# Cross attention scores on one Trainium2 core: full-height products against pairs of half-height products

## What is computed

```
q = xn2 @ Wq_c + bq_c                 # per sequence 16 heads x 1024 x 32
k = ctx @ Wk_c + bk_c                 # per sequence 16 heads x   64 x 32
v = ctx @ Wv_c + bv_c
scores = (q @ k.T) / DH ** -0.5       # 16 heads x 1024 x 64
attn = softmax(scores, axis=-1)
x = x + (attn @ v) @ W2 + b2
```

## Time and profile before

| | us |
|---|---|
| median of 3 runs (lowest, highest) | 2375.3 (2372.14, 2384.62) |
| the profiled execution: its time | 2376.49 |
| the profiled execution: its span | 2374.7 |
| TensorE (matmuls) busy | 2223.8 (94%) |
| weight loads busy, beside the matmuls | 1606.6 (68%) |
| VectorE, ScalarE, GpSimd busy | 1414.0, 867.5, 934.5 |
| mean granted TensorE clock, share of full speed | 0.971 |

### The profile page before, as it was taken

How to read it: one execution, slowest core, us unless ns; L and a number is a source line. 1 busy time by engine, 2 the same in 40 slices (tenths; PEclk the granted TensorE clock), 3 DMA queues, 4 the chain that set the end, 5 groups by cost and what they waited for, 6 DMA issues and landing times.

```text
span 2374.7 us, 31670 instructions
## 1 busy us (share of the span) xinstructions
PE 2223.8 (94%) x11334; PEld 1606.6 (68%) x11334; DVE 1414.0 (60%) x3348; ACT 867.5 (37%) x1598; POOL 934.5 (39%) x943
## 2 busy tenths in 40 slices
PE   6999999999999999878999998999999999999996
PEld 4665565556555655436777776788887887788784
DVE  4377757775777566745666667553446545554636
ACT  3145645554556455443333434221112121121213
POOL 1057666666677667773433333110112202021212
PEclk9999999989999999799999999999999999999998
DMA  7265544544455346321121112321111111211011
GB/s 231 29 90 85 104 66 78 92 91 66 77 96 97 66 78 96 104 72 49 68 80 54 58 54 76 116 85 54 36 67 58 67 62 54 94 54 67 32 36 49
DMA packets 106321, 177.31 MB, mean 75 GB/s; under 512 B 18334, under 2 KB 23454, under 8 KB 106160
## 3 DMA queue, kind: packets, MB, share of 16 engines
q1 hardware_dynamic: 106164, 175.29, 31.0%
HBM read 83.67 MB, written 40.13 MB: 52 GB/s over the span
## 4 chain that ended last, share of the span: by engine, by line
PE 75%; DVE 9%; issue 6%; ACT 4%; POOL 3%; DMA 2%; SPq 0%; POOLq 0%; ACTq 0%; DVEq 0%
PE psum L55 18%; PE psum L56 17%; PE psum L57 17%; PE psum L793 5%; PE psum L743 5%; PE psum L781 4%; PE psum L701 1%; PE psum L802 1%; DVE psum L995 1%; POOL es L658 1%; PE psum L754 1%; ACT sx L1342 1%; DMA ks<-stage 1%; PE psum L1296 1%; PE psum L720 1%
## 5 line engine op out<-in xcount | busy, mean ns | idle before, releaser
L658 POOL TENSOR_TENSOR es<-es,er 128x512 f32<-128x512 f32 (+3 forms) x640 | 589.6, 958 | 346.4 <-PE psum L793 305.8
L891 ACT ACTIVATE er<-psum 128x512 f32<-128x512 f32 (+3 forms) x640 | 279.8, 470 | 327.7 <-DVE psum L1006 191.4
L995 DVE CUSTOM_DVE_ANT_0 psum<-psum,mask_ts 128x384 f32<-128x384 f32 (+3 forms) x512 | 248.7, 502 | 231.3 <-PE psum L743 230.1
L743 PE MATMUL psum<-ks,qs 96*128 96x512 f32 (+3 forms) x768 | 270.8, 378 | 22.4 <-DMA ks<-stage 11.0
L781 PE MATMUL psum<-qs,ks 100*128 100x512 f32 (+3 forms) x768 | 261.9, 375 | 18.3 <-DVE mx L999 9.9
L1846 ACT ACTIVATE fy<-psum,cols 128x512 f32<-128x512 f32 x128 | 88.2, 689 | 453.2 <-PE psum L57 452.6
L743 PEld LDWEIGHTS psum<-ks,qs 96*128 96x128 f32 x768 | 145.6, 197 | 123.4 <-issue 48.8
L999 DVE TENSOR_REDUCE mx<-psum 128x1 f32<-128x512 f32 x256 | 175.4, 685 | 68.2 <-PE psum L743 67.6
L781 PEld LDWEIGHTS psum<-qs,ks 100*128 100x128 f32 x768 | 145.7, 196 | 92.5 <-DVE mx L999 24.2
L55 PE MATMUL psum<-fh,hh 128*128 128x512 f32 x512 | 201.1, 393 | 7.1 <-DVE hl L1947 7.1
L55 PE MATMUL psum<-fah,fh 128*128 128x512 f32 x512 | 203.4, 397 | 0.0
(11 more groups left out here) (257 smaller groups left out, 4507.4 us busy)
## 6 DMA issues: line engine op xcount, KB each, us to landing
qs<-stage SPq DMA_DIRECT2D x96, 256.0 KB, 5.6
ks<-stage SPq DMA_DIRECT2D x96, 256.0 KB, 6.7
rs<-rs_d SPq DMA_DIRECT2D x32, 256.0 KB
sa_d<-rs SPq DMA_DIRECT2D x32, 256.0 KB, 2.1
sx<-sa_d SPq DMA_DIRECT2D x8, 1024.0 KB, 5.6
xt<-in_x SPq DMA_DIRECT2D x32, 256.0 KB, 5.9
x_d<-xt SPq DMA_DIRECT2D x32, 256.0 KB, 2.0
fw<-in_Wf SPq DMA_DIRECT2D x16, 512.0 KB, 5.3
```

The lines of the kernel that those rows point to most:

```text
L658: e.tensor_tensor(es, es, er, ALU.add).then_inc(s_add.sem, 1)
L743: t = e.matmul(bank1(*s)[:, v * wd:v * wd + wd], Q.qs[par][0:96, i, 128 * ti:128 * ti + 128], Q.ks[par][0:96, i, c0:c0 + wd], start=True, ...
L891: e.activation(dst, bank1("sc", g, c2, j, i)[:, off:512], ACT.Exp, scale=SCALE).then_inc(s_freeS.sem, 1)
L995: t = e.tensor_tensor_reduce(out=ps, in0=ps, in1=mask_ts[:, 512 - wd:512], scale=1.0, scalar=-3e38, op0=ALU.add, op1=ALU.max, accum_out=mx ...
```

## The change

Each score product over 128 partitions and 256 columns becomes two over 64 partitions and 128 columns each. Half `a` (partitions 64a to 64a+63) holds heads 2a and 2a+1 of the group, its block diagonal is 128 columns wide, and its scores go to bank 3 + a, at columns 128m. The two halves are issued in turn. `kbh` and `kbl` are half as wide, and a gap of 4096 floats per partition keeps all later buffers where they were. Since the banks now hold the heads in another order, `place(h)` gives the place of head h, and the transposes of `2tu` read `pp` from there. All waits, increments and planned times stay as they were.

```diff
-            R.kbh = sb(ctx, "kbh", [128, NB, 4, 256], F32R)
-            R.kbl = sb(ctx, "kbl", [128, NB, 4, 256], F32R)
+            R.kbh = sb(ctx, "kbh", [128, NB, 4, 128], F32R)
+            R.kbl = sb(ctx, "kbl", [128, NB, 4, 128], F32R)
+            sb(ctx, "gap2", [128, 4096])
...
+        def place(h):
+
+            return 8 * (h // 2 % 2) + 2 * (h // 4) + h % 2
...
-                t = three(e, bank[3 + m // 2][:, 256 * (m % 2):256 * (m % 2) + 256], (R.qh[qp][:, m, r], R.ql[qp][:, m, r]),
-                          (R.kbh[:, b, m, :], R.kbl[:, b, m, :]), True, True)
+                for z, (lhs, rhs) in enumerate(((R.qh, R.kbh), (R.qh, R.kbl), (R.ql, R.kbh))):
+                    for a in range(2):
+                        pair = slice(64 * a, 64 * a + 64)
+                        t = e.matmul(bank[3 + a][:, 128 * m:128 * m + 128], lhs[qp][pair, m, r], rhs[pair, b, m, :], start=z == 0, stop=z == 2)
...
-                    h = 2 * (4 * hf + v)
+                    h = place(2 * (4 * hf + v))
...
-                    e.activation(R.kbh[r, :, m, 64 * i:64 * i + 64], bank[(1 + m) % 2][r, 0:256].rearrange("p (b s) -> p b s", s=S),
+                    e.activation(R.kbh[r, :, m, 64 * (i % 2):64 * (i % 2) + 64], bank[(1 + m) % 2][r, 0:256].rearrange("p (b s) -> p b s", s=S),
...
-                    dh, dl = (q[r, :, m, 64 * i:64 * i + 64] for q in (R.kbh, R.kbl))
+                    dh, dl = (q[r, :, m, 64 * (i % 2):64 * (i % 2) + 64] for q in (R.kbh, R.kbl))
```

## The result

The changed kernel takes 2384.75 us (median of 20 runs, 2372.03 to 2393.10), the kernel before 2378.64 us in as many runs beside it (2365.39 to 2384.62): ratio 1.0030, 95% interval 1.0019 to 1.0042. That is 7 us, between 4.5 and 10: slower by a hair, within what was called no change. The forecast was 2385 us and a loss of 9.5 us. That 2385 was met to 0.3 us is luck: the forecast started from 2375.3 us, and the kernel before took 3.3 us more beside the changed one, which made up for a loss some 3 us smaller than forecast. The loss is what the forecast is to be judged by.

What follows compares the result with a forecast made beforehand. The prediction took TensorE as the bound: 32 short runs +11.2 us, their pairs -1.9, runs of 12 +0.2, together +9.5 on the median of 2375.3, giving 2385 us; range 2370 to 2421.

Steps and rivals of the forecast that it cites:

- What is worked on: Score products between 1095 and 1510 us: 12 per tile at 0.120 us, 32 tiles, 46 us or 1.9% of the kernel.
- A pair in 0.11 us: Two half products with their loads take 0.11 us, 0.01 less than the full product; 192 pairs in short runs: -1.9 us.
- 0.35 us per run: Entering and leaving a run of half products costs 0.35 us; 32 short runs, not covered: +11.2 us.
- Runs of 12 covered by their stalls: In 16 tiles with one run of 12, leaving falls into TensorE's existing stall of some 0.47 us; taken: +0.2 us.
- The sum, +9.5 us: All terms together: 9.5 us added to the median of 2375.3 us, giving 2385 us.
- lower end: Forecast case's range, 2379 to 2390 us; its low side allows part to fall into TensorE's waits for GpSimd and ScalarE.
- a microsecond added to TensorE is a microsecond of the kernel: TensorE, busy 94% of the span, is the bound; added time counts fully unless it falls where TensorE waits.
- Clearing and filling: Clearing `kbh` and `kbl` takes about 1.75 us each instead of 3.5; filling the diagonals is unchanged; both gain nothing.
- Loads queue: Rival: the two halves' loads use one path, a pair takes 0.22 us; total +44 us, 2420 us; chance 0.27.
- No change over: Rival: a split by partitions costs nothing to enter; -4 us, 2371 us; chance 0.12.
- free of the load: Rival: a pair takes only its columns' 0.06 us; -23 us, 2352 us, or 2363 with change overs; chance 0.04.
- Doesn't do what it says: Rival: halves run without any overlap, or the change over costs double, 0.7 us per run; +22 us, 2397 us; chance 0.10.

Runs made afterwards that it cites:

- the lower half twice: Changed kernel with the upper half's products replaced by the lower half's, made a second time into the upper half's bank: 2423.2 us, ratio 1.0201.
- one run per tile: Changed kernel with the four score steps of each tile planned next to one another, 32 runs of score products instead of 48: 2380.6 us, ratio 1.0013.
- high by high only: Two remainder products left out, 4 score products or pairs per tile instead of 12: kernel before 2365.0 us (0.9965), changed kernel 2374.0 us (0.9996).
- the half kernel: Changed kernel with each tile's score steps planned together, right before the value products: 2409.4 us (1.0139); kernel before on the same plan 2391.6 us (1.0069).

## Why the prediction was right

- **What is worked on.** "46 us is all that the change works on": held; outside the stretch nothing moved that doesn't move between profiles of one kernel or of kernels with full products too.
- **A pair in 0.11 us.** Held, by the timeline (0.11) and by the sum over runs. It was taken from column splits and applies to row splits. That it rests on the loads of two halves running side by side is shown by the lower half twice, where as many loads on one half take twice as long.
- **0.35 us per run.** Measured: 0.31 to 0.32 net for six couples and 0.32 to 0.33 net for three. With 0.01 per couple given back this is 0.36 to 0.38, so the term was up to 10% short. How much of it is draining and how much are loads that no longer run ahead, no experiment separates. That it is a price of the run and not of the couples is shown by one run per tile (16 runs fewer, 5.7 us less in the timelines, 6 in the time) and by the kernels with high by high only.
- **Runs of 12 covered by their stalls.** Held in the main. Before a W1 product the piece around one took 2.00 us before and after. Before value products it grew by 0.05 to 0.16, about 1 us in eight tiles, where the sum had 0.2: this term was too small.
- **The sum, +9.5 us.** Added up in the timeline, runs and stalls give 9.7 + 1 us. The stretch grew by 8.7 us at the same clock, for the most part since two of TensorE's waits shrank: for `pp` from 8.8 to 7.7 us and for `xt` from 2.3 to 1.4. The prediction named waits that shrink when TensorE is late, and left them in its lower end. The time grew by 7 us (4.5 to 10), a quarter less than the forecast; the interval takes in the stretch's 8.7, so whether the step "a microsecond added to TensorE is a microsecond of the kernel" loses more outside is not shown.
- **Clearing and filling.** `kbh` is cleared in 1.80 us instead of 3.5, with nothing behind it to gain.
- **Rivals.** "Loads queue" would have cost what the lower half twice costs, and is excluded. "No change over" and "free of the load" are excluded by the timeline (0.32 us per run, 0.11 per couple). "Doesn't do what it says" likewise: the halves do overlap, and a run's ends cost 0.36 to 0.38 us, not 0.7. That is why the gain stays so small: side by side, two half products cost one load time, 0.11 us, and the full product had cost 0.12.

The Trainium skill, "TensorE: Matmul & The Clock Gate", section on LDWEIGHTS, says that a load's time goes by its columns and that loading fewer rows is no quicker. The trace agrees: 0.188 us for a load of 64 partitions, 0.190 for 128.

## What to carry to other kernels

Before splitting a product to use the array better, ask what sets its pace now: with weights new for every product, a 128 column load (0.11 us) was already the whole cost of a 256 column product (0.12 us), and halving the columns had 0.01 us to give. Each unbroken run of split products pays some 0.36 us at its ends, so a run would need some 36 couples to earn it back at this rate (an estimate from 0.36 and 0.01), unless the run lies in front of a stall; count runs, not products, and join them first, or put them next to products that are split already. And a step that fills a stall is worth more than its own time: moved away, it opened a gap of 1.9 us per chunk, and in the half kernel the clock fell behind it as well.

## What was not expected of the hardware

Products for different halves need not alternate in the program. With three products of one half ahead they still ran in couples (12 couples from first start to last in 1.29 us); with twelve ahead only three overlapped (24 products in 2.23 us).

Two neighbouring runs with different splits, scores by rows and values by columns, share the change over between them: halving the score products cost 0.06 us per run there, and 0.25 between full products.

With the same plan and the same idle 1.88 us, the granted clock fell to its lower level in the profile of the half kernel (0.57 over 8 us), and not in that of the full one.
